# Turning u on VectorE in the loop of a two-layer token kernel, and moving two products in TensorE's order

## The reference, cut to what matters

```
base   = x @ W.T
logits = x @ Wr.T + 5 * one_hot(language)
gates  = softmax over the two largest logits, 0 elsewhere
y      = base + 2 * sum_e gates[e] * (x @ A[e].T) @ B[e].T
g2     = softmax(y @ Wr2.T)
out    = x + y @ W2.T + b + 2 * sum_e g2[e] * (y @ A2[e].T) @ Bm[e].T
```

## Time and profile before

| | us |
|---|---|
| median of 3 runs | 324.22 (324.12 to 325.24) |
| the profiled execution | 324.05 |
| its span, first to last instruction | 322.5 |
| PE busy in the span | 319.0 (99%) |
| PEld busy | 312.8 (97%) |
| DVE busy | 245.2 (76%) |
| ACT busy | 128.0 (40%) |
| granted TensorE clock | 1.000 |

### The profile page before, as it was taken

How to read it: one execution, slowest core, us unless ns; L and a number is a source line. 1 busy time by engine, 2 the same in 40 slices (tenths; PEclk the granted TensorE clock), 3 DMA queues, 4 the chain that set the end, 5 groups by cost and what they waited for, 6 DMA issues and landing times.

```text
span 322.5 us, 5962 instructions
## 1 busy us (share of the span) xinstructions
PE 319.0 (99%) x2255; PEld 312.8 (97%) x2255; DVE 245.2 (76%) x540; ACT 128.0 (40%) x253; POOL 1.4 (0%) x11
## 2 busy tenths in 40 slices
PE   8999999999999999999999999999999999999996
PEld 5999999999998999899999999999999999999996
DVE  4989999998799778988866856757575695665543
ACT  4972836495148236225413503411431340342111
POOL 1000000000000000000000000000000000000000
DMA  7998000000000311700430340160042025003003
GB/s 283 417 405 273 2 2 0 2 0 2 0 2 0 132 35 35 260 3 0 137 127 0 81 179 0 20 240 0 0 151 109 0 65 195 0 0 130 0 0 130
DMA packets 10702, 27.55 MB, mean 85 GB/s; under 512 B 3166, under 2 KB 4702, under 8 KB 10688
## 3 DMA queue, kind: packets, MB, share of 16 engines
q1 hardware_dynamic: 10256, 26.83, 23.4%
q10 hardware_dynamic: 432, 0.53, 0.5%
HBM read 18.97 MB, written 8.39 MB: 85 GB/s over the span
## 4 chain that ended last, share of the span: by engine, by line
PE 98%; DMA 1%; DVE 0%; issue 0%
PE sums L1277 97%; DMA in<-part 1%; PE sums L1516 1%; DVE rows L1054 0%; DVE b_high L782 0%
## 5 line engine op out<-in xcount | busy, mean ns | idle before, releaser
L1277 PE MATMUL sums<-b_high,a_high 128*128 128x256 f32 (+1 forms) x224 | 45.6, 287 | 0.2 <-DVE b_high L782 0.2
L1277 PE MATMUL sums<-b_low,a_high 128*128 128x256 f32 (+1 forms) x224 | 45.3, 286 | 0.0
L1277 PE MATMUL sums<-b_high,a_low 128*128 128x256 f32 (+1 forms) x224 | 45.2, 285 | 0.0
L1277 PEld LDWEIGHTS sums<-b_high,a_high 128*128 128x128 f32 x224 | 34.8, 190 | 1.2 <-ACT a_high L533 1.0
L1277 PEld LDWEIGHTS sums<-b_low,a_high 128*128 128x128 f32 x224 | 34.7, 189 | 0.0
L1277 PEld LDWEIGHTS sums<-b_high,a_low 128*128 128x128 f32 x224 | 34.7, 188 | 0.0
L1054 DVE TENSOR_TENSOR narrow<-sums,narrow 128x244 f32<-128x244 f32 x30 | 12.4, 412 | 25.7 <-PE sums L1277 25.6
L1054 DVE TENSOR_TENSOR rows<-sums,rows 128x354 f32<-128x354 f32 x48 | 24.4, 522 | 9.7 <-PE sums L1277 9.3
L1277 PE MATMUL sums<-t_high,s_high 128*128 128x354 f32 x96 | 31.6, 329 | 0.0
L1277 PE MATMUL sums<-t_low,s_high 128*128 128x354 f32 x96 | 31.1, 324 | 0.0
L1277 PE MATMUL sums<-t_high,s_low 128*128 128x354 f32 x96 | 31.1, 324 | 0.0
(11 more groups left out here) (149 smaller groups left out, 821.8 us busy)
## 6 DMA issues: line engine op xcount, KB each, us to landing
stage<-tokens SPq DMA_DIRECT2D x14, 512.0 KB, 4.1
out<-rows SPq DMA_DIRECT2D x14, 512.0 KB, 5.1
in<-part SPq DMA_DIRECT2D x7, 585.0 KB, 7.9
in<-part SPq DMA_DIRECT2D x4, 777.0 KB, 14.7
in<-part SPq DMA_DIRECT2D x4, 265.0 KB, 17.1
rows<-tokens SPq DMA_DIRECT2D x2, 512.0 KB, 13.4
out<-rows SPq DMA_DIRECT2D x3, 192.0 KB, 2.3
c_plain<-gate_proj SPq DMA_DIRECT2D x1, 544.0 KB, 18.6
```

The source lines that it names most:

```text
L1277: return nc.tensor.matmul(out_, lhs, rhs, start=start, stop=stop, skip_group_check=True)
```

## The change

In the pairs of the loop, except the last pair (`turning`, five pairs, 2 to 6), VectorE turns u: sixteen transposes of 32 by 64 (both tiles at once), written to columns 0 to 63 of each half of `narrow`, whose projections have been read by then. `ut_high` and `ut_low` are made from there. On VectorE `add_u3` and `add_r22` move up around `ut_low`, S4 and the low part of S2 move down into the chain to v, and the low part of S3 moves behind the tails and the two additions after them. On ScalarE the rounding of the next pair's first tile moves ahead of `ut_high`. On TensorE the two turning matmuls go, wide product 5 goes ahead of `small_y`, and wide product 3 ahead of `mixed_tails`. The last pair keeps the old order, and is written out on TensorE behind the loop.

```diff
@@ ScalarE, pair @@
+                if steady and not last:
+                    act.wait_ge(p2_done, j + 1)
+                    round_x(j + 1, 0)
                 act.wait_ge(u_turned, j + 1)
-                copy(ut_high[:, :, :], ut_psum).then_inc(ut_high_ready, 1)
+                if steady and not last:
+                    copy(halves_of(ut_high), ut_plain).then_inc(ut_high_ready, 1)
+                else:
+                    copy(ut_high[:, :, :], ut_psum).then_inc(ut_high_ready, 1)
...
-                if steady and not last:
-                    act.wait_ge(p2_done, j + 1)
-                    round_x(j + 1, 0)
@@ VectorE @@
+            def turn_u(j):
+
+                dve.wait_ge(u_ready, j + 1)
+                for i in range(P // BLOCK):
+                    at = slice(i * BLOCK, (i + 1) * BLOCK)
+                    for q in range(P // BLOCK):
+                        rows_at = slice(q * BLOCK, (q + 1) * BLOCK)
+                        ins = nc.vector.transpose(ut_plain_at(at, q * BLOCK, BLOCK), u[rows_at, :, at])
+                ins.then_inc(u_turned, 1)
...
                 add_sums(rows[:, 0, wide_at(1)], bank(BANK_B), rows[:, 1, wide_at(0)]).then_inc(u2_read, 1)
-                if steady:
-                    next_s(S4)
-                    if not last:
-                        split_s(j + 1, S2)
+                if turning:
+                    turn_u(j)
+                    add_u3()
 
                 dve.wait_ge(ut_high_ready, j + 1)
-                low_part(ut_low[:, :, :], ut_psum, ut_high[:, :, :]).then_inc(ut_low_ready, 1)
+                if turning:
+                    low_part(halves_of(ut_low), ut_plain, halves_of(ut_high)).then_inc(ut_low_ready, 1)
+                else:
+                    low_part(ut_low[:, :, :], ut_psum, ut_high[:, :, :]).then_inc(ut_low_ready, 1)
+                if turning:
+                    add_r22()
...
-                if second:
+                if second or turning:
                     next_s(S4)
...
                 ins.then_inc(v_turned, 1)
 
-                if steady:
+                if turning:
+                    split_s(j + 1, S2)
+                if last:
                     add_r22()
...
-                if steady and not last:
-                    split_s(j + 1, S3)
...
                 add_sums(rows[:, 1, wide_at(0)], bank(BANK_B), rows[:, 1, wide_at(0)]).then_inc(b_out, 1)
+                if turning:
+                    split_s(j + 1, S3)
                 if not last:
                     split_x(j + 1, 1)
@@ TensorE, pair @@
-                if steady:
+                if last:
                     turn_u()
...
                 of_s(BANK_B, S3, t_high[T3], t_low[T3], False).then_inc(p7_done, 1)
+                if turning:
+                    product_5(j)
                 if steady:
                     small_y()
                 lora(BANK_A, 0, 0)
+                if second or last:
+                    product_5(j)
...
                 of_x(BANK_B, 1, 1, t_high[T4], t_low[T4], False).then_inc(p4_done, 1)
+                if turning:
+                    lora(BANK_B, 1, 0)
+                    product_3(j)
+                    mixed_tails(j)
+                elif last:
+                    mixed_tails(j)
+                    lora(BANK_B, 1, 0)
...
                 mixed(BANK_B, 1, 0).then_inc(b_done, 1)
-
-                pe.wait_ge(s_split, 4 * j + 4)
-                pe.wait_ge(r22_read, j + 1)
-                of_s(BANK_C, S4, cw_high[B22], cw_low[B22], False).then_inc(p3_done, 1)
+                if not turning:
+                    product_3(j)
...
-            with pe_loop(2, PAIRS) as j:
+            with pe_loop(2, PAIRS - 1) as j:
                 pair(j)
+            pair(PAIRS - 1, last=True)
```

More of the change, by code:

```diff
@@ L421, in narrow_of, with ut_plain_at, halves_of @@
             return c_plain[:, c, :, GATE_AT:HB]
+        ut_plain = narrow[:, :, :, 0:P // 2]
+        def ut_plain_at(partitions, c, n):
+            h, c = divmod(c, P // 2)
+            return narrow[partitions, :, h, c:c + n]
+        def halves_of(t):
+            return t[:, :, :].rearrange("p t (h c) -> p t h c", h=2)
         def stored_at(h):
@@ L1057, in _ @@
             BLOCK = 32
+            def turn_u(j):
[6 more added lines that the diff above has]
+                ins.then_inc(u_turned, 1)
             def pair(j, first=False, second=False, last=False):
                 steady = not first and not second
+                turning = steady and not last
                 base = STEPS * j + VEC_START
@@ L1154, in pair @@
                     split_block(B21, C21)
[L1156 to L1160, removed]
-                if steady:
-                    next_s(S4)
-                    if not last:
-                        split_s(j + 1, S2)
-                dve.wait_ge(ut_high_ready, j + 1)
-                low_part(ut_low[:, :, :], ut_psum, ut_high[:, :, :]).then_inc(ut_low_ready, 1)
-                if first:
-                    split_t(T4, C11)
-                if second:
[L1171 to L1176, removed]
                 def add_u3():
@@ L1189, in add_r22 @@
                     add_sums(rows[:, 1, wide_at(1)], bank(BANK_C), rows[:, 1, wide_at(1)]).then_inc(r22_read, 1)
-                if steady:
+                if not first:
+                    dve.wait_ge(stored[0], 16 * j)
+                dve.wait_ge(r1_read, j + 1)
+                dve.wait_ge(p6_done, j + 1)
+                add_sums(rows[:, 0, wide_at(1)], bank(BANK_B), rows[:, 1, wide_at(0)]).then_inc(u2_read, 1)
+                if turning:
+                    turn_u(j)
+                    add_u3()
+                dve.wait_ge(ut_high_ready, j + 1)
+                if turning:
[4 more added lines that the diff above has]
+                    add_r22()
+                if first:
+                    split_t(T4, C11)
+                if second:
+                    split_tn(T2)
+                    make_tn(C11, C21, C11, t4n_made)
+                    next_s(S1)
+                    next_s(S2)
+                    next_s(S3)
+                if last:
                     add_u3()
@@ L1471, in narrow_products, with product_3, pair @@
                 narrow_of_s(BANK_NC, S4, cn_high[B22], cn_low[B22], False).then_inc(p3n_done, 1)
-            def pair(j, first=False, second=False):
+            def product_3(j):
+                pe.wait_ge(s_split, 4 * j + 4)
+                pe.wait_ge(r22_read, j + 1)
+                of_s(BANK_C, S4, cw_high[B22], cw_low[B22], False).then_inc(p3_done, 1)
+            def pair(j, first=False, second=False, last=False):
                 steady = not first and not second
+                turning = steady and not last
                 s_no = S_NO_FIRST if first else S_NO
@@ L1531, in pair @@
                 of_x(BANK_A, 0, 1, cw_high[B21], cw_low[B21], False).then_inc(p2_done, 1)
-                if steady:
+                if last:
                     turn_u()
-                else:
+                if not steady:
                     small_y()
@@ L1553, in pair @@
                 of_x(BANK_B, 1, 1, t_high[T4], t_low[T4], False).then_inc(p4_done, 1)
-                if not steady:
+                if turning:
[5 more added lines that the diff above has]
+                    lora(BANK_B, 1, 0)
+                else:
                     lora(BANK_B, 1, 0)
                     mixed_tails(j)
-                else:
-                    mixed_tails(j)
-                    lora(BANK_B, 1, 0)
                 mixed(BANK_A, 0, 0).then_inc(a_done, 1)
```

1 line of the change is left out of this document (removed).

## The result

| | before | after |
|---|---|---|
| median of 8 runs each, us | 324.31 (324.12 to 325.24) | 325.43 (324.91 to 325.88) |
| ratio to before, 95% interval | | 1.0026 (1.0015 to 1.0038) |
| profiled execution, its span | 324.05, 322.5 | 325.38, 324.1 |
| granted TensorE clock | 1.000 | 0.999 |

The changed kernel is slower by about 1.1 us, a third of a per cent. The forecast was no change (324.2). The measured time lies in the range and within the 0.5% of the prediction, but the interval of the ratio leaves 1 out, so there is something to explain.

The account below looks back on a forecast made before the run. TensorE was taken as the bound: each pair -0.22 + 0.08 + 0.13 = -0.01 us, five of them -0.05, giving 324.0 profiled and, with the median 0.17 above it, 324.2 us; range 323.0 to 325.6.

Parts of the forecast that it names:

- What bounds the kernel, and the gain: TensorE, busy throughout a 27.31 us pair, is the bound; dropping two turning matmuls saves 0.22 us in each of five pairs.
- The sixteen transposes: On VectorE, turning u by blocks starts every 0.246 us and takes 3.92 us a pair.
- rival (b): Sixteen transposes slower than v's because of their strides, so the small columns wait; at 0.28 us a block 326.8; chance 0.10.
- First handover: `ut_low` from VectorE to TensorE's small columns: gap 0.11 us, cost between 0.03 and 0.19, taken as 0.08 a pair.
- Second handover: Tails' addition on VectorE to the next pair's first narrow product: gap 0.12 us, loss 0.02 to 0.18, taken as 0.13.
- the two waits: At the next pair's start the product waits in code for `tails_out` and `x_split`, the reason given for taking 0.13 us.
- Third and fourth: VectorE's queue before narrow product 7 (0 to 0.07 us, taken as nothing); second tile's later load before narrow product 3 (covered).
- rival (c): Second tile lands late, narrow product 3 waits 0.36 to 0.52 us in four pairs, 1.4 to 2.1 in all; chance 0.08.
- rival (d): One engine does not do as said: TensorE loses the gain at the loop's exit, in one stall, size unbounded; chance 0.04.
- The written-out last pair: TensorE leaving its loop into more code: nothing to a single stall, taken as nothing.
- What is added on VectorE: Sixteen transposes, 3.92 us, raise VectorE from 18.4 to 22.3 us of 27.3; other moved work costs only its place.

Follow-up runs that it names:

- one_more: The changed kernel with a seventeenth transpose of the same form ahead of the sixteen, its result overwritten later; 326.13 us in one run.
- tails_early: The changed kernel with `lora(BANK_B)` moved behind `mixed_tails`, three matmuls more between the tails and the next pair; 325.14 us, ratio 1.0014 to the kernel before.
- after_again: The changed kernel, unedited, run again with a second profile; 325.74 us, ratio 1.0037 to the kernel before.
- peel_only: The kernel before with only TensorE's last pair written out behind its loop; 324.71 us, ratio 1.0008.
- pad_end: The kernel before with sixteen small VectorE instructions in the last pair that write to unused memory; 325.01 us, ratio 1.0014.
- after_slim: The changed kernel with VectorE's program 14 instructions shorter, in the first multiplication and a counter; 324.27 us, ratio 0.9989 to the kernel before.
- p5_back: The changed kernel with product 5 back behind the small columns and lora(BANK_A) in the loop; 341.69 us in one run.

## Why the prediction was right and wrong

**What bounds the kernel, and the gain: right.** TensorE bounds it, and the two turning matmuls are worth 0.22 a pair: with the handovers taken away, pairs are 27.09 to 27.10, from 27.31.

**The sixteen transposes: right.** 3.97 us against 3.92, mean 236 ns against 232 for v's. The strides don't matter here, and rival (b) falls. Its condition was the right one: a little more in this place is paid one for one in each pair (one_more). That the transposes cost more of VectorE (3.97 us) than the matmuls of TensorE (0.22) held; it didn't decide.

**First handover: mechanism right, term mis-sized.** Said 0.08, measured 0.15 in pairs 4 to 6. The need came out as taken (0.16, in the 0.14 to 0.21 of the prediction): TensorE's next start was due at 230.85 (230.69 and 0.163), `ut_low` ended at 230.84, and 0.15 were lost. The gap, 0.11 by my sum, is 0.01: the transposes took 0.05 more, and the steps behind them a little each. A sum of some ten steps was good to 0.10 us, and the term it gives was no larger than that.

**Second handover: right in kind.** Said 0.13, measured 0.10. Both together cost 0.25 in a steady pair where 0.21 was said, and a pair of 27.33 to 27.34 lies in the 27.25 to 27.35 that the prediction named. But it was said for five pair starts, and the last pair, which stands outside TensorE's loop, doesn't have it: there the addition ends 0.13 us ahead of the first matmul, as at the four others, yet the weight load follows it after 0.05 instead of 0.12, and the second matmul is 0.02 late instead of 0.10. So the 0.10 needs the late tails (tails_early) and the turn of TensorE's loop as well. The prediction put the longer need down to the two waits; the last pair has both waits too.

**Third and fourth, rival (c), rival (d): right but for a remainder.** No wait at narrow product 7. The second tile lands late and S1 waits up to 0.9 for it, as said. The waits of the changed kernel:

```profile
DVE s_plain L898 <- DMA stage<-tokens: 3.9, 5, 0.9
```

In four of its five pairs nobody behind S1 is in need. In pair 3 S1 starts 7.12 us behind the pair's start (6.79 was said), and the addition of R22 behind it ends 0.17 ahead of narrow product 3. The timelines of VectorE and of TensorE there:

```profile
191.78 0.41 DVE L1068 TENSOR_TENSOR narrow<-sums,narrow 128x244 f32<-128x244 f32 x1
...
192.36 0.32 PE L1308 MATMUL sums<-ct_high,s_high 128*128 128x244 f32 x1
192.52 0.28 PE L1308 MATMUL sums<-ct_low,s_high 128*128 128x244 f32 x1
```

The second matmul comes 0.16 behind the first instead of 0.11. That is rival (c) in small, 0.05 us in all (0.08 and 0.05 in two pairs of after_again) where 1.4 to 2.1 was put on it.

The written-out last pair of TensorE costs nothing (peel_only).

**The step that failed** is "What is added on VectorE. Sixteen transposes." They were costed at their duration and at nothing besides. They are also 1,024 B more of VectorE's program, and with them a second load of instructions falls beside the last store: +0.52 and +0.96 at the end in the two profiles of the changed kernel. The clean test is pad_end, which has the same size of program and none of the change: +0.91 at the end and +0.54 in the medians, the largest single term. With the program short again (after_slim) the end is -0.01. So for the end the cause is shown twice, by adding it alone and by taking it away.

**The second miss is in the loop**, +0.33 and +0.40 in the two profiles where the steps of the prediction give -0.05. Most of it is the 0.25 us that pair 2 waits longer at the small columns than the others: the first handover was sized on the rows of pair 4, and the pause of pair 2, which the kernel before has too, stood in no term. The rest is the mis-sized first handover and the remainder of (c). With the pause gone (after_slim) the loop is +0.02, and the median is 0.4 us under the kernel before; with it, and with the second load, +1.1. That the measured time lies in the stated range all the same is luck: the range reached up to 325.6 for the sake of rival (c), which cost 0.05.

The row that could have told is the one of queue 14 from the last 3 us of the kernel before, shown above: a load 0.14 us behind the landing of the last store. I read the chain, which ends with that store, and never asked what else shares the DMA engines then, nor how near the next load of VectorE's program stood.

What stays open: where in the program a load is due (14 instructions fewer in an early stage were enough; the boundary itself wasn't sought), whether the pause of pair 2 is a wait for instructions (it goes and the load moves when the program is shorter, but no row names its cause), why the time exceeds the span by 0.23 us less with the second load, and what is left between the accounts of single profiles and the medians.

## What to carry to other kernels

An added instruction has two prices, its duration on its engine and its length in that engine's program. Where a kernel ends in a store, look at the instruction loads around it before and after: here half a microsecond hung on some sixteen instructions, added in the loop or in the last pair, or taken away in the first stage. And where work moves to a free engine, order the consumer so that what doesn't need the last piece stands in front of what does: that turned 0.25 us of handover a pair into nothing here, and together with the shorter program made of a loss of 0.3% a gain of 0.3%.

## What the hardware showed that was not expected

- An 8 KB load of VectorE's instructions meets the last store and delays one of its sixteen parts, and with it the end of the span, by 0.5 to 1.0 us (end 3.43 to 3.91 in nine profiles, without it 2.89 or 2.90 in five). The Trainium skill, *Runtime: NRT & Kernel Launch*, "Instruction fetch mechanics", says that the cost of fetching the next block is mostly hidden. Where TensorE's two loads more fall, 20 us and more ahead of the end, the traces agree (peel_only, at 291 and 300 us, pairs and end unchanged); at the end of this kernel they don't.
- A wait costs more than its length: the weight load starts 0.05 us (ut_low) or 0.12 us (tails, at the turn of TensorE's loop) behind VectorE's end, and the second matmul is then 0.10 late, even where the first one is on time. Outside the loop the same tails cost 0.02.
- After gaps of 1.84 to 2.09 us in TensorE the granted clock fell to 0.50 for 3 us in two of five pairs, both behind a gap of 1.84, 1.5 us each (p5_back).
